# Layer-norm statistics by strips in one bank: means and factors go through DRAM, no centring matmuls, four banks for tiles

## What is computed

```python
q = silu(causal_dwconv(hidden_states @ Wq, qconv_w, qconv_b))      # 16 heads of 128
k = silu(causal_dwconv(hidden_states @ Wk, kconv_w, kconv_b))
m = jnp.mean(x, axis=-1, keepdims=True)
var = jnp.mean((x - m) ** 2, axis=-1, keepdims=True)
q, k = (x - m) * lax.rsqrt(var + eps) * w + b                      # each head of q and of k
S = (1.0 - b) * S + b * (v_t[..., :, None] * k_t[..., None, :])    # scan over time
o_t = jnp.einsum('bhvk,bhk->bhv', S, q_t)
x = x + (o * silu(hidden_states @ Wg)) @ Wo                        # then adapter, ternary FFN
```

## Time and profile before

| | us |
|---|---|
| median of 3 runs | 2686.22 (2684.64 to 2687.25) |
| the profiled execution's own time | 2685.08 |
| its span, first to last instruction | 2683.5 |

### The profile page before, as it was taken

The page is one execution under the profiler, slowest core; times in us unless marked ns, Lnnn a source line. Parts: engine busy times, 40 slices in busy tenths (PEclk is TensorE's granted clock), DMA queues, the critical chain, the costliest instruction groups (busy, mean ns, idle before and its releaser), DMA issues.

```text
span 2683.5 us, 39968 instructions
## 1 busy us (share of the span) xinstructions
PE 2556.3 (95%) x14536; PEld 1985.0 (74%) x14536; DVE 1688.5 (63%) x2848; ACT 1197.7 (45%) x1878; POOL 696.3 (26%) x764
## 2 busy tenths in 40 slices
PE   5889999999999999999999999999999999999996
PEld 4667777777777777777777777777777777777774
DVE  3766666666666666666656666666666666666653
ACT  3555544544444444354444444353444544444431
POOL 3465522212222212222212222222212212222220
PEclk8999999999999999999999999999999999999998
DMA  6775745445444555355354454444544445444540
GB/s 167 249 224 185 240 154 159 139 155 177 121 142 147 165 166 157 109 172 194 113 173 132 144 177 154 151 139 138 163 148 156 140 149 179 120 146 142 171 132 16
DMA packets 264554, 416.17 MB, mean 155 GB/s; under 512 B 102058, under 2 KB 126634, under 8 KB 264362
## 3 DMA queue, kind: packets, MB, share of 16 engines
q1 hardware_dynamic: 264362, 413.63, 48.6%
HBM read 360.86 MB, written 52.69 MB: 154 GB/s over the span
## 4 chain that ended last, share of the span: by engine, by line
PE 88%; DVE 4%; ACT 3%; issue 2%; SPq 1%; POOL 1%; DMA 0%; ACTq 0%; DVEq 0%; POOLq 0%
PE ring L1048 31%; PE pj_a L1048 26%; PE pj_b L1048 13%; PE ring L1264 4%; PE m L1254 3%; PE var L1222 2%; PE cen_q L1243 2%; PE cen_k L1243 1%; PE cen_k L1244 1%; PE cen_q L1244 1%; PE ring L1149 1%; PE ring L1066 1%; ACT hb L912 1%; PE var L1233 1%; PE m L1264 1%
## 5 line engine op out<-in xcount | busy, mean ns | idle before, releaser
L780 DVE SCALAR_TENSOR_TENSOR y_q<-pj_a,conv,y_q 128x504 f32<-128x504 f32 (+2 forms) x384 | 281.7, 734 | 360.2 <-ACT y_q L963 351.0
L498 POOL TENSOR_TENSOR og_lo<-gt,og_hi 128x512 fp32r<-128x512 f32 x128 | 165.1, 1290 | 922.3 <-ACT og_hi L993 922.3
L1048 PE MATMUL pj_a<-ht_hi,wg 128*128 128x512 f32 x1024 | 352.9, 405 | 2.2 <-DVE y_q L780 2.1
L1048 PE MATMUL pj_a<-ht_hi,wq 128*128 128x512 f32 x1024 | 345.0, 398 | 2.5 <-DVE ht_lo L626 1.5
L1048 PE MATMUL pj_b<-ht_hi,wk 128*128 128x512 f32 x1024 | 335.9, 389 | 0.0
L1048 PE MATMUL ring<-wo,og_hi 128*128 128x512 f32 x1024 | 321.5, 395 | 14.8 <-DVE acc L660 11.8
L1048 PE MATMUL ring<-wv,ht_hi 128*128 128x512 f32 x1024 | 320.8, 394 | 6.8 <-ACT hb L914 6.8
L780 DVE SCALAR_TENSOR_TENSOR y_k<-pj_b,conv,y_k 128x504 f32<-128x504 f32 (+2 forms) x384 | 281.8, 734 | 62.3 <-ACT y_k L963 53.2
L951 ACT ACTIVATE sq_q<-cen_q 128x512 f32<-128x512 f32 x128 | 76.7, 599 | 435.7 <-PE cen_q L1244 435.7
L1048 PEld LDWEIGHTS ring<-wo,og_hi 128*128 128x128 f32 x1024 | 190.4, 189 | 74.2 <-DVE acc L660 18.5
L1048 PEld LDWEIGHTS ring<-wv,ht_hi 128*128 128x128 f32 x1024 | 189.2, 188 | 74.0 <-issue 26.8
(11 more groups left out here) (202 smaller groups left out, 5084.4 us busy)
## 6 DMA issues: line engine op xcount, KB each, us to landing
wq<-parts_q SPq DMA_DIRECT2D x112, 512.0 KB, 4.1
wk<-parts_k SPq DMA_DIRECT2D x112, 512.0 KB, 4.5
wg<-parts_g SPq DMA_DIRECT2D x112, 512.0 KB, 3.7
wv<-parts_v SPq DMA_DIRECT2D x112, 512.0 KB, 6.4
wo<-parts_o SPq DMA_DIRECT2D x112, 512.0 KB, 6.1
keep<-keep_rows SPq DMA_DIRECT2D x256, 64.0 KB, 3.9
wo<-parts_w SPq DMA_DIRECT2D x28, 512.0 KB, 5.6
acc<-in_x_dram SPq DMA_DIRECT2D x8, 1024.0 KB, 5.5
```

The source lines that it names most:

```text
L498: G.tensor_tensor(og_lo[:, u % OG_RING, :], gt[:, u % GT_RING, :], og_hi[:, u % OG_RING, :].bitcast(F32), ALU.subtract).then_inc(S["oglo"], 1)
L780: V.scalar_tensor_tensor(out=yy[:, :, k:], in0=pp[:, :, :L - k], scalar=conv[:, i, h, 3 - k:4 - k], in1=yy[:, :, k:], op0=ALU.mult, op1=AL ...
L1048: last = T.matmul(psum, a, b, start=start and n == 0 and m == 0, stop=stop and n == len(pairs) - 1 and m == 2)
```

## The change

- `centre`, `silu_hi`, `silu_lo`, `keep_centred`, `rstd_hi`, `split_rstd` and `spread` are gone, with the banks `cen_q`, `cen_k`.
- `means`: once for two units, in even slots behind the projection of q, four matmuls with 32 output rows put the means of two q and two k into the strips of one bank, `stat`. ACT copies the bank to `rstd` (`keep_means`), writes the four rows to DRAM (8 KB) and, when that write has landed (`spread_means`), issues four DMAs that each read one row back to all 128 partitions of `sq` (256 KB each).
- DVE subtracts the mean of q (`centre_q`), POOL that of k (`centre_k`), in place in `y`, which becomes a ring of five. ACT squares from there, four squares at once behind the gate of the even slot.
- `variance` moves to odd slots, into the same bank `stat`; `seed` and `newton` follow in that slot. The factors go the same way: `keep_rstd` writes four rows, `spread_rstd` reads them back with four DMAs. Both stand on ACT ahead of `gate`, and the DMAs of this path are all issued by ACT.
- `normalise` of both units stands at the start of the next even slot, `affine` behind it. Scores, attention and everything after them come one slot later (U-4 for U-3), and the program has one slot more.
- Four banks (`ring0` to `ring3`) take the tiles. The table of tiles, the splits of the first group and SP's loads of Wv, Wo and the dense weights are spread anew over the slots.

```diff
-    3: ([("v", 0, 0, 2), ("v", 0, 0, 3)], [("o", -1, 3, 0)]),
-    4: ([("o", -1, 3, 1)], [("o", -1, 3, 2), ("o", -1, 3, 3)]),
+    3: ([("v", 0, 0, 2)], [("v", 0, 0, 3)]),
+    4: ([("o", -1, 3, 0)], [("o", -1, 3, 1)]),
...
-OG_RING, GT_RING, C_RING = 6, 4, 3
+OG_RING, GT_RING, Y_RING, TILE_RING = 7, 5, 5, 4
...
-    SLOTS = UNITS + 4
+    SLOTS = UNITS + 5
...
+    m_rows = nc.dram_tensor("m_rows", [4, GROUP], F32).ap()
+    r_rows = nc.dram_tensor("r_rows", [4, GROUP], F32).ap()
...
-        cen = {"q": bank("cen_q"), "k": bank("cen_k")}
-        var = bank("var")
+        stat = bank("stat")
...
-        ring = [bank("ring0"), bank("ring1")]
+        ring = [bank(f"ring{i}") for i in range(TILE_RING)]
...
+            def centre_k(u):
...
+                pool.wait_ge(S[f"m_in_k{u % 2}"], 16 * (u // 2 + 1))
+                c = y["k"][:, u % Y_RING, :]
+                G.tensor_tensor(c, c, sq["k"][:, u % 2, :], ALU.subtract).then_inc(S["c_k"], 1)
...
+            def keep_means(m):
+                act.wait_ge(S["mean_made"], m + 1)
+                if m:
+                    act.wait_ge(S["r_out"], 16 * m)
+                A.activation(rstd[:], stat[:], ACT.Identity).then_inc(S["mean_kept"], 1)
+                act.wait_ge(S["mean_kept"], m + 1)
+                for j in range(4 if m else 0):
+                    act.wait_ge(S[f"m_in_{'qk'[j % 2]}{j // 2}"], 16 * m)
+                act.dma_start(m_rows, rstd[0:P:32, :]).then_inc(S["m_out"], 16)
+
+            def spread_means(m):
+                act.wait_ge(S["m_out"], 16 * (m + 1))
+                for j in range(4):
+                    x_ = "qk"[j % 2]
+                    if m:
+                        act.wait_ge(S[f"n_{x_}"], 2 * m - 1 + j // 2)
+                    act.dma_start(sq[x_][:, j // 2, :], m_rows[j:j + 1, :].broadcast_to([P, GROUP])
+                                  ).then_inc(S[f"m_in_{x_}{j // 2}"], 16)
+
+            def keep_rstd(m):
+                act.wait_ge(S["rr"], m + 1)
+                for j in range(4 if m else 0):
+                    act.wait_ge(S[f"r_in_{'qk'[j % 2]}{j // 2}"], 16 * m)
+                act.dma_start(r_rows, rstd[0:P:32, :]).then_inc(S["r_out"], 16)
+
+            def spread_rstd(m):
+                act.wait_ge(S["r_out"], 16 * (m + 1))
+                for j in range(4):
+                    x_ = "qk"[j % 2]
+                    act.dma_start(sq[x_][:, j // 2, :], r_rows[j:j + 1, :].broadcast_to([P, GROUP])
+                                  ).then_inc(S[f"r_in_{x_}{j // 2}"], 16)
...
             for U in range(SLOTS):
                 if U < UNITS:
                     project("q", U)
+                if U % 2 == 0 and 2 <= U <= UNITS:
+                    means(U // 2 - 1)
+                if U < UNITS:
                     project("k", U)
-                if U % 2 == 0 and 2 <= U <= UNITS:
-                    variance(U // 2 - 1)
-                if U % 2 and 0 <= U - 2 < UNITS:
-                    spread(U - 2)
+                if U % 2 and 3 <= U <= UNITS + 1:
+                    variance((U - 3) // 2)
                 make(U, 0)
-                if 0 <= U - 3 < UNITS:
-                    score(U - 3)
+                if 0 <= U - 4 < UNITS:
+                    score(U - 4)
                 if U < UNITS:
                     project("g", U)
                 make(U, 1)
-                if U % 2 == 0 and 2 <= U <= UNITS:
-                    spread(U - 2)
-                if 0 <= U - 3 < UNITS:
-                    attend(U - 3)
-                if U < UNITS:
-                    centre("q", U)
-                    centre("k", U)
+                if 0 <= U - 4 < UNITS:
+                    attend(U - 4)
```

270 lines of the change are left out of this document (110 added, 160 removed), and 27 rows, old and new, of tables (END_TILES, SLOT_TILES, SPLIT_PARTS).

## The result

The changed kernel takes 2639.6 us (median of 4 runs, 2635.6 to 2642.2) against 2686.5 of the kernel before: ratio 0.983, 95% interval 0.981 to 0.984. It is faster by 46.8 us, where 131 was forecast; the time lies at the very end of the stated range, 2515 to 2640.

A forecast was written before the change was run, and what follows sets the result against it. PE was taken as the bound, by its number of matmuls (busy 2556.3 of 2683.5 us). Terms -106 - 34 - 12 + 8 + 8 + 6 = -130 us gave 2555 us, range 2515 to 2640.

The forecast's parts named there:

- Centring, spreading, means: Matmuls on PE: centring out -119 us, spreading out -64, means in +77, together -106 us.
- Waits that go: PE's waits for the split factors (23.3 us) and the low part of silu of k (11.0) vanish: -34 us.
- The first group: In the stretch with the most DMA, added reads land later and hold ACT: +8 us, bounds 0 and +33.
- first group gets slower: Rival: queues fill in the first group, weights come late and all 33 us are lost: 2590 us, chance 0.07.
- a first group that takes as long as before: Sign named in advance that, seen in the profile after, would show the prediction wrong.
- Four banks: Tiles' waits for a bank DVE or ACT had yet to empty shrink: -12 us, bounds 0 and -21.
- The gate behind DMAs: In odd slots ACT's gate follows a write and four issues, 1.4 us ahead of PE: +8 us, bounds 0 and 77.
- ACT is held longer: Rival: small write lands after 4 us or more, or issues exceed 0.63; every second slot waits: 2600 to 2660 us, chance 0.13.
- slower than before: Rival: the gate's path in odd slots is long enough to eat the whole gain: about 2750 us, chance 0.07.
- The end: From the end of slot 127 to the last output tiles, 33.0 us against 28.6: +6 us, bounds +2 and +14.
- Traffic: The broadcasts add 2 MB for two units, 134 MB over the run on top of 413.63.

The follow-up runs named there:

- oldtab2: Changed kernel with the tile table, first-group splits and SyncE load places of the kernel before, and two tile banks instead of four: 2733.1 us.
- g0_narrow: Changed kernel with first-group broadcasts of means and factors loading 64 columns instead of 512, same writes, issues and waits: first group 330.6 us against 329.1.
- oldtab4: Changed kernel with the tile table, first-group splits and SyncE load places of the kernel before, keeping four tile banks: 2603.6 us.
- ring2: Changed kernel with two banks for tiles instead of four, new table kept: 2773.8 us.
- all_narrow: Changed kernel with all broadcasts of means and factors, in every group, loading 64 of 512 columns: 2621.2 us, settled groups 307.3 us.
- g0_nosave: Changed kernel with split weights saved and loaded for 16 of 128 partitions only: first group 307.0 us against 329.1, settled groups 304.6 us.

## Why the prediction was wrong, point by point

- **Centring, spreading, means (-106).** Right as a count of matmuls. PE's busy time is 88.4 us lower at a clock of 0.969 for 0.986. In the first group without DMAs it fell by 13.6 us for 16 units, 0.85 each, for 0.83. The step of the means is 1.00 us (1300.72 to 1301.72):

```profile
1300.72 0.62 PE L1218 MATMUL stat<-y_q,mean 128*32 128x512 f32 x1
...
1301.72 0.50 PE L1046 MATMUL pj_b<-ht_hi,wk 128*128 128x512 f32 x1
```

- **Waits that go (-34).** The waits went, the time did not. In the first group PE's idle time without any of the new DMAs was 31.5 us for 23.2: instead of losing 20 us it gained 8. Of that the new table and the new split places hold a part: with those of before the first group was 15.3 us shorter, DMAs and all. One place, the late raw weight, is 8.9 us of it. And that the time of these matmuls comes back in full did not hold without the banks: with two of them (oldtab2) the change is 46 us slower than before.
- **The first group (+8, bounds 0 and +33). This is the step that failed.** The DMAs there cost 36.1 us, and the bound was no bound: it was the gain that the group could lose, 13 + 20, and nothing keeps a loss within a gain. With the 28 us by which 293.0 misses the 265 that the forecast had without its +8, the group came out 64 above those 265. What the path left out are the parts that hold only there: the write took 2.8 to 3.3 us in most of its odd slots for the 1.6 of a quiet place, the splits of the weights stood between it and the gate, and VectorE waited 31.2 us for the broadcasts. The rival "first group gets slower" had the right place and half the size, but not the reason: it had the queues fill up by the new bytes, and these cost nothing (g0_narrow). Its sentence on a second issuer, from the Trainium skill, "DMA: Bandwidth & Descriptors", section "Issuing engines are not separate DMA queues", agrees with slot 9: ScalarE's write took about 5 us behind SyncE's 2 MB, and 1.7 ahead of them. The prediction also said what to look for, "a first group that takes as long as before", and it took longer.
- **Four banks (-12, 0 to -21).** Wrong as a price by a factor of ten (-130 by oldtab2 and oldtab4, -134 by ring2), and yet not what moved the total: I read their worth from the waits of before, and the change itself made the banks scarce. Two terms that depend on each other were summed as if they did not. That the change came out faster at all is luck here: the four banks, priced at 12 us, were worth 130, and without them it is slower than before.
- **The table** had no term at all. It was taken to be free; it costs 36 us, more than the four smallest terms together.
- **The gate behind DMAs (+8, 0 to 77).** The path was right to 0.1 us in the write (1.7 for 1.6) and better in the issues (0.45 for 0.63). The gate still cost 57.5 us, for reasons that the path did not hold: in the first group splits and late raw weights, and in slot 9 a write that landed late behind four weight loads, with five ScalarE operations of tiles ahead of the gate. The rival "ACT is held longer" had this condition, a small write that lands after 4 us or more, but for every second slot; it was seven places and a start. (In the rival "slower than before" the issues would have to take 1.5 us and not 1.2: 7.7 less 1.6 for the write, over four.)
- **The end (+6).** The last stretch is 11.8 us longer in respect to a settled group (395.9 - 308.7 against 397.6 - 322.2). From the last scores to the first output tile I took 6.2 us; in the changed kernel it is 11.1 (2562.47 to 2573.60), and the kernel before had it already (2607.96 to 2619.44, 11.5). A row for it was to be had.
- **Traffic (2 MB a pair).** Right that it costs little when settled: 1.4 us a group, by all_narrow, and 14 in all. The weights' own traffic costs more, 4.1 us a group by g0_nosave.

The Trainium skill, "DMA: Bandwidth & Descriptors", section "Latency and other measured facts", with its 2 us for HBM at high load, was weighed as the rule against the change. The writes of about 5 us in slot 9 and of 8.9 in the first group are well beyond it. In slot 9 the small write pays for the large transfers ahead of it, as the fall to 3.0 or less with an eighth of their bytes shows; for the 8.9 us no run does. The trace decides.

## What to carry to other kernels

A DMA round trip put into an engine's fixed order costs its latency at the *worst* place of the program, and reading its size from a quiet place prices only that place; price it per stage, and look at what stands in the queues ahead of it. A long wait with a slow DMA in front of it need not be that DMA's: take the DMA out and see what is left (8.9 of 9.8 us here), and before a moved tile is called the cause, look at which loads wait for it. Matmuls that are removed have covered something: before adding up waits of the old profile, ask which of them the removed work kept short. And a table that comes with a change wants a term of its own; here the old one with the new banks was 36 us better, and eight small loads issued in three places instead of one another 33.

## What the runs showed of the hardware

- A DMA that reads one SBUF partition 128 times lands in 21.3 us (11.8 to 32.6) where the same 256 KB from a DRAM row take 4 to 6; 13.91 MB took 63% of 16 engines for 600 us.
- A DRAM write of 8 KB landed in 1.7 us in a settled odd slot, in 4.9 to 5.6 when SyncE had issued 2 MB of loads in the 2 us before it (slot 9), and in 3.0 or less there when those loads had an eighth of the bytes (g0_nosave). In the first group one took 8.9 us, in a spell in which all transfers were slow.
- That spell, some 9 us below 100 GB/s, came in the changed kernel and in the one before, each time behind four stores of 512 KB and a DRAM write of 2 KB (which took 12.9 us itself in the changed kernel); raw weights of 256 KB issued in it took 10.4 and 11.2 us. Its cause is not shown.
- VectorE's multiplication of 128x512 took 1.76 us for 0.68 while GpSimd ran, both as tensor-tensor operations (139.90 in the first group of the changed kernel, against 1301.15; GpSimd's splits beside it took 1.72 for 1.27).
- Eight small loads whose addresses are read from a register cost SyncE 9.25 us, 1.16 each, against 0.33 to 0.63 for a plain load of 512 KB.
